# One more wait in the edge passes: GpSimd waits, at the fourth gather of a group of five, for the landing of the group before

## The reference: what is computed

```python
# L0: edge messages, maximum by destination
h = relu(concat([x[dst], x[src] - x[dst]]) @ W1 + b1);  out = segment_max(h @ W2 + b2, dst)
# L1: mean of edge attributes by source, then a two-layer MLP on the nodes
v_e = segment_sum(edge_attr, src) / max(cnt, 1)
# L2: mean of neighbours by destination, then a gate and a linear layer
h = segment_sum(x[src], dst) / max(deg, 1)
# L3: typed attention with 4 heads: k, v by source and edge type, q by destination, softmax over dst
a = (kw * qw).sum(-1) * rel_pri / sqrt(d);  alpha = softmax_by_dst(a);  h = segment_sum(m * alpha, dst)
```

## Time and profile before

| | |
|---|---|
| Median of 3 runs | 21968.09 us (21966.59 to 21971.33) |
| Span of the profiled execution | 21982.3 us |
| Pass b, first to last gather | 6288.5 to 11054.3 us |
| Pass c, first to last gather | 11484.3 to 15843.6 us |
| Pass d, first to last gather | 16782.2 to 21555.0 us |
| POOL busy | 69% |
| DVE busy | 31% |

### The profile page before, as it was taken

How to read it: one execution, slowest core, us unless ns; L and a number is a source line. 1 busy time by engine, 2 the same in 40 slices (tenths; PEclk the granted TensorE clock), 3 DMA queues, 4 the chain that set the end, 5 groups by cost and what they waited for, 6 DMA issues and landing times. The chain is left out here.

```text
span 21982.3 us, 148548 instructions
## 1 busy us (share of the span) xinstructions
PE 4774.0 (22%) x30182; PEld 4149.9 (19%) x30182; DVE 6911.8 (31%) x16401; ACT 1772.2 (8%) x6281; POOL 15097.0 (69%) x13304
## 2 busy tenths in 40 slices
PE   4444444444423333333320000000041000000002
PEld 4444444444412222222210000000031000000001
DVE  3333333333312222222241111111122444444444
ACT  1111111111100000000010000000021000000001
POOL 5888888888876666666657777777724666666664
PEclk8555555555555555555555555555576555555555
DMA  4444444444422222222231111111122222222222
GB/s 93 53 52 52 52 52 53 50 53 52 52 48 65 65 65 65 63 65 64 65 59 48 47 47 46 47 47 46 43 68 89 87 89 89 87 90 87 89 89 38
DMA packets 1456154, 1380.95 MB, mean 63 GB/s; under 512 B 777810, under 2 KB 1260924, under 8 KB 1455996
## 3 DMA queue, kind: packets, MB, share of 16 engines
q0 software_dynamic: 775408, 541.25, 17.1%
q1 hardware_dynamic: 662716, 736.98, 10.3%
q10 hardware_dynamic: 18000, 102.41, 1.1%
HBM read 762.18 MB, written 617.56 MB: 63 GB/s over the span
## 5 line engine op out<-in xcount | busy, mean ns | idle before, releaser
L500 POOL DMA_INDIRECT agg<-sums,ag_idx x3125 | 4984.9, 1595 | 1166.4 <-issue 1118.5
L534 POOL DMA_INDIRECT gat<-tab_t,gi x3125 | 3021.6, 967 | 1752.5 <-issue 928.0
L534 POOL DMA_INDIRECT gat<-tab_b,gi x3125 | 3014.6, 965 | 1752.6 <-issue 931.3
L534 POOL DMA_INDIRECT gat<-tab_x,gi x3125 | 3299.2, 1056 | 1100.9 <-issue 1061.1
L842 PE MATMUL bank<-at,same 128*128 128x64 f32 x6250 | 1882.7, 431 | 3281.7 <-issue 1057.3
L842 PEld LDWEIGHTS bank<-at,same 128*128 128x128 f32 x6250 | 1570.5, 311 | 3419.7 <-issue 1813.5
L908 PE MATMUL pair<-ident,tails 128*64 128x128 f32 (+1 forms) x20 | 4.9, 419 | 9304.2 <-DVE tails L1209 4931.4
L908 PEld LDWEIGHTS pair<-ident,tails 128*64 128x64 f32 (+1 forms) x20 | 3.0, 167 | 9305.2 <-DVE tails L1209 4931.6
L1302 DVE TENSOR_TENSOR run_sb<-p,gat 128x320 f32<-128x320 f32 x625 | 317.1, 507 | 3710.6 <-DMA gat<-tab_x,gi 3710.6
L1164 DVE TENSOR_TENSOR run_sb<-p,bank 128x320 f32<-128x320 f32 x625 | 304.9, 488 | 3177.7 <-remote 2346.6
L876 PE MATMUL bank<-ident,ub 128*128 128x128 f32 x1250 | 413.0, 434 | 3494.1 <-DVE ub L1192 2228.1
(11 more groups left out here) (263 smaller groups left out, 13806.5 us busy)
## 6 DMA issues: line engine op xcount, KB each, us to landing
edge<-start_rows SPq DMA_DIRECT2D x250, 800.0 KB
run<-run_sb SPq DMA_DIRECT2D x250, 800.0 KB
run<-run_sb SPq DMA_DIRECT2D x125, 900.0 KB
start_rows<-zeros ACTq DMA_DIRECT2D x125, 800.0 KB, 3.5
at<-in_edge_attr SPq DMA_DIRECT2D x125, 800.0 KB
tab_t<-trow SPq DMA_DIRECT2D x98, 512.0 KB, 2.6
agg<-sums,ag_idx POOLq DMA_INDIRECT x3125
gat<-tab_b,gi POOLq DMA_INDIRECT x3125
```

What stands on the lines that cost most here:

```text
L500: pool.indirect_dma_start(agg_d[r], rows(agg_d[r], ag_idx[:, k, r:r + 1]), sums[:, k, r, :], None, bounds_check=AGR - 1, oob_is_err=True, ...
L534: pool.indirect_dma_start(gat[:, k, s, 0:width], None, table, rows(table, gi[tp][:, s, k:k + 1])).then_inc(g_in[c][k], 16)
```

## The change

In the loop over the five gathers of a group, at `s == 3`, GpSimd gets a wait: for groups `k` = 1 to 4 until all five gathers of group `k - 1` of the same tile have landed, for `k` = 0 (except in the first tile) until those of the last group of the tile before have. A no-operation follows it, as it follows the other waits. It is in the one function for all three passes.

```diff
                         for s in range(SUB):
+                            if s == 3 and k:
+                                pool.wait_ge(g_in[c][k - 1], t * (16 * SUB) + 16 * SUB)
+                                pool.nop(nofuse=True)
+                            elif s == 3 and not first:
+                                pool.wait_ge(g_in[c][KS - 1], t * (16 * SUB))
+                                pool.nop(nofuse=True)
                             pool.indirect_dma_start(gat[:, k, s, 0:width], None, table,
                                                     rows(table, gi[tp][:, s, k:k + 1])).then_inc(g_in[c][k], 16)
```

## The result

| | before | changed |
|---|---|---|
| Median | 21967.22 us (20 runs, 21957.8 to 21981.93) | 22007.21 us (20 runs, 21990.65 to 22044.23) |
| Ratio | | 1.0019, 95% interval 1.0013 to 1.0026 |
| Span of the profiled execution | 21982.3 us | 22000.6 us |
| Pass b, first to last gather | 4765.9 us | 4779.2 us |
| Pass c | 4359.3 us | 4355.4 us |

The forecast was 19,960 us. Nothing of the 2060 us that were to go went.

What follows compares the result with a forecast made beforehand. GpSimd was taken to be held at the ring's end by readers whose hand-overs its long gather queue slowed. Savings of 821.3 + 824.5 + 414.4 = 2060.2 us, less 52 back, gave 19,960 us; range 19,850 to 21,350.

Steps and rivals of the forecast that it cites:

- the 2060 us that were to go: Passes b, c, d: predicted saving of 821.3 + 824.5 + 414.4 = 2060.2 us, before some 52 us come back.
- What bounds the kernel: Passes b and d: GpSimd, needing about 3946 us a pass, idles 821.3 and 824.5 us at the five-group ring's limits.
- the length of the queue of gathers handed over and not begun: GpSimd in b, c, d: inferred cause of the slow semaphore hand-overs; shortening it was to save 2060.2 us.
- The control from stage a: Stage a: short queue, POOL busy 81%, longest DVE scatter wait 5.6 us, no slow spells; taken to support the queue cause.
- The term of c: Pass c: mean gather and its gap return to those of b, saving 414.4 us, bounds 0 and 425.
- The added wait: Fourth gather in b, c, d: 1872 waits hidden at cost 0, upper bound 505 us if the engine runs dry.
- The 2.5 us of room: Fourth gather: the landing wait is over 2.5 us before the engine needs that gather, 5.0 us after the last gather's start.
- The no-operation: Sequencer instruction after the added wait: cost 0 while work is queued, otherwise within the 505 us.
- No change: Rival for the passes: slow spells come from the loops, as delays of reading instructions in; time 21,968 us, chance 0.11.
- by itself, whatever GpSimd holds: Claim within the no-change rival: instruction-reading delays at fixed loop places would stall each engine independently of GpSimd; 21,968 us.
- The rule of the Trainium skill: GpSimd's engine queue: 8 entries, so the chip would already hold it about as short and the time would stay.
- Slower: Rival, mainly pass c: landings seen later than 5.0 us make GpSimd run dry at the new wait; 22,300 us, chance 0.11.

Runs made afterwards that it cites:

- e1_nop: Kernel before with only the no-operation at the fourth gather, without the wait, where no hand-overs were slow: 19878.6 us, 1.0001.
- e14: Kernel before plus a small memset that GpSimd's sequencer waits for before every group, emptying its queue, where hand-overs were slow: 21589.39 us, 0.9826.
- e19: Kernel before with GpSimd allowed two groups ahead of the one being read instead of four, where hand-overs were slow: 21467.05 us, 0.9782.
- e18: Kernel before, unedited, as a program of its own, where hand-overs were slow: 21957.11 us, 1.0001.
- e17: Changed kernel, unedited, measured again against the kernel before, where hand-overs were slow: 21977.69 us, 1.0015.
- e8: Changed kernel's wait moved from the fourth gather to the third, against the kernel before, where no hand-overs were slow: 20460.08 us, 1.0300.
- e16: Kernel before with only the no-operation at the fourth gather, without the wait, where hand-overs were slow: 21948.17 us, 0.9997.
- e6: Changed kernel's wait moved from the fourth gather to the first, against the kernel before, where hand-overs were slow: 23974.7 us, 1.0825.
- e7: Changed kernel's wait moved from the fourth gather to the second, against the kernel before, where hand-overs were slow: 22009.44 us, 0.9939.
- the first and second sets: First two groups of experiment runs, each read against its own kernel before: 19,876 us without slow hand-overs, then 22,149 us with them.
- e4_body4: Kernel before with loop bodies of four tiles instead of two, where no hand-overs were slow: 19883.32 us, 1.0003.
- e13: Changed kernel's wait moved from the fourth gather to the third, against the kernel before, where hand-overs were slow: 21838.53 us, 0.9941.
- e15: Kernel before with GpSimd allowed one group ahead of its reader instead of four, where hand-overs were slow: 21492.19 us, 0.9782.
- the drain: Kernel before plus a memset waited for before every group, emptying GpSimd's queue: 1.0756 without slow hand-overs, 0.9826 with them.
- the fourth: Group of runs with slow hand-overs, of wait at third gather, drain, lead of one and changed kernel; kernel before 21,974 us.

## Why the prediction was wrong

- **What bounds the kernel: right.** Idle at the ring's end, not GpSimd's own work, stands between the kernel and some 3950 us a pass; e1_nop and its neighbours run at 3977, 3928 and 3981. The 20,000 us that I reached for exist, but the unedited code reaches them in other surroundings, and this change doesn't.
- **"So it isn't GpSimd's work that disturbs the others but, as I read it, the length of the queue of gathers handed over and not begun": this is the step that failed.** It was called an inference, with no row under it. The changed kernel has a queue of 4 at most (at the head of a group) and as many slow steps; e14 with at most 3 has them in b; e1_nop with 12 has none; e19 with 8 gains 2.2%. All 2060 us of the sum hung on it.
- **The control from stage a: true, but it proves nothing.** GpSimd's queue is short there, 3 scatters in the median and at most, and so is the changed kernel's, which has slow hand-overs. Nor is it a pause that keeps stage a free of them: 3,124 of its 3,125 scatters follow after the bare gap of 0.31 us. What differs is that they are scatters, begun every 1.85 us in the median instead of every 1.25; no run varied that. One "control" that differs in several ways from the case couldn't single out the queue's length.
- **The term of c, 414.4 us: right size, wrong cause.** Where hand-overs are quick, c takes 3928 us in place of 4359, 431 less; the wait changes nothing in it.
- **The added wait, 0 of 0 to 505 us: nearly right.** It measured 26 to 40 us in three comparisons and 16 us, unclear from zero, in a fourth; in the traces of e18 and e17 it is 97 us of longer gaps at the fourth gather, over half of them covered. The 2.5 us of room were right in the median: in the changed kernel GpSimd passes the new wait 2.5 us in b, 2.6 in c and 2.4 in d before the fourth gather is due, and only in 19 of 1,872 groups after the third has ended. With 1.25 us less room (e8) it cost 3%.
- **The no-operation, 0: right** (0.9997 and 1.0001).
- **The rivals.** "No change" named the right time, for a reason that isn't settled. In d of e18 (as of the kernel before and e16) the slow steps fall on the same two of the ten groups of a loop body in 62 of 62 iterations, which looks like the loops. But in the changed kernel, whose readers' code is the same, those two have 21 each of 169 slow steps, and in e19 they are spread evenly; with the pauses of e6 and e7 they are gone. So it isn't true that each engine stalls "by itself, whatever GpSimd holds". Reading of instructions isn't excluded by that (see the last section); the instruction queues moved 30 packets in the whole run, in the kernel before as in e1_nop. The rule of the Trainium skill that I set against myself, 8 entries in GpSimd's queue ("TensorE: Matmul & The Clock Gate"), would have given the right time too, but not by what the trace shows: the queue stood at up to 12, over the page's 8, went down to 4, and the time stayed. "Slower" had the right sign and place, fourth gathers that see a landing late, at a tenth of its price.

The range began at 19,850 and ended at 21,350: it left out "no change" though the whole gain hung on an unseen quantity. One question would have changed the chances: what else is different in stage a?

## What stays open

Why the same program has slow hand-overs in some sets and none in others. It isn't the chip as such: one chip showed both, in the first and second sets. Nor could the place in the code be tested, as e4_body4 met a set without them. That pauses or a shorter lead help because GpSimd stops sooner is argued from five kernels with one sign (e7, e13 to e15, e19), not shown by itself; stage a, without a pause and without slow hand-overs, says that it isn't the whole. And the changed kernel was never measured in a set without them, so what its wait costs there is unknown.

## What to carry to other kernels

When a gain hangs on a quantity that no row shows, look first for one that the trace does give (here, the sequencer's passing of its waits against the engine's starts), and put the chance of "no change" where that inference stands. If a producer is stopped again and again at the end of its ring while its readers have time to spare, try a shorter lead: it is one constant, and it gained 2.2% where hand-overs were slow (a lead of one lost 1.2% where they weren't; the lead of two wasn't measured there). Price such an edit in both surroundings, since the drain was 7.6% slower in the one and 1.7% faster in the other.

## What the hardware showed that I had not expected

- One program, unedited, takes 19,865 us or 21,952 to 22,149 us, 10 to 11% apart, and keeps to one value through all its runs of a set (21,953 to 21,981 in 15 runs of the fourth).
- The difference is in the passes in which GpSimd streams gathers. SyncE's register and branch instructions in pass c take 41 ns in the mean in e1_nop and some 800 in the kernel before; in stage a they take 42 to 44 in both, and in c those of DVE, ACT and POOL stay at 36 to 46 in both. The long ones stand at a few fixed places, above all the loop's end, in every iteration; the register instruction at the store itself (L395) stays at 44 in both. Two rows of L408 in pass c (duration in ns, least/median/most), of the kernel before and then of e1_nop:

```profile
L408 SPq COMPARE_BRANCH  x61: 704/1397/1411, 11552.6 to 15743.9; - x61
L408 SPq FUSED_REGOPS  x60: 687/697/708, 11555.4 to 15678.7; - x60
...
L408 SPq COMPARE_BRANCH  x61: 44/49/54, 10761.7 to 14533.7; - x61
L408 SPq FUSED_REGOPS  x60: 41/41/41, 10762.0 to 14471.7; - x60
```

- So instructions that wait for no other engine are slow as well, and they too are quick again with pauses: 41 ns in the mean in c of e6 and e7, 43 in c of e14. In pass d some of DVE's take over 600 ns: 13 before, 101 in e19, none in e1_nop.
- In c the gathers themselves are longer, 1056 ns against 953 in the mean, at a median of 945 and 944.
- POOL's sequencer is up to 12 gathers ahead of its engine (before, e1_nop).
